# Experts in 64 full and 8 mixed slots, rows padded to 64, with each expert's weights as one long row per partition

## The reference

```python
cw = _combine_weights(xt, gate_w)           # [T, 16], 4 entries of a row are not zero
out = jnp.zeros_like(xt)
for e in range(16):
    a = _swiglu(xt @ expert_up_w[e].T)      # 512 -> 2 * 352 -> 352
    out = out + cw[:, e:e + 1] * (a @ expert_down_w[e].T)   # 352 -> 512
out = out + _swiglu(xt @ shared_up_w.T) @ shared_down_w.T
```

## Time and profile before

| | us |
|---|---|
| median of 3 runs (lowest, highest) | 1310.31 (1309.14, 1313.19) |
| span of the profiled execution | 1306.4 |
| PE busy | 1264.5 (97%) |
| DVE busy | 872.4 (67%) |
| ACT busy | 375.1 (29%) |
| POOL busy | 340.0 (26%) |
| TensorE clock over the span, of full speed | 0.989 |

### The profile page before, as it was taken

The page is one execution under the profiler, slowest core; times in us unless marked ns, Lnnn a source line. Parts: engine busy times, 40 slices in busy tenths (PEclk is TensorE's granted clock), DMA queues, the critical chain, the costliest instruction groups (busy, mean ns, idle before and its releaser), DMA issues.

```text
span 1306.4 us, 27873 instructions
## 1 busy us (share of the span) xinstructions
PE 1264.5 (97%) x8725; PEld 787.1 (60%) x8726; DVE 872.4 (67%) x2430; ACT 375.1 (29%) x822; POOL 340.0 (26%) x398
## 2 busy tenths in 40 slices
PE   8969999999999999999999999999999999999997
PEld 7857778777775555444444555555555555555553
DVE  4897688768768465262111777777777777777774
ACT  4745655645553333210000111111111111111111
POOL 1301234313242231225651112121212122121212
PEclk9989999999997999999999999999999999999999
DMA  5524944743643694585467456666665656564420
GB/s 163 95 47 99 157 94 101 166 105 85 138 109 114 169 199 116 124 274 199 182 211 246 85 130 138 134 137 137 137 139 133 135 132 136 127 139 72 75 49 9
DMA packets 208516, 171.09 MB, mean 131 GB/s; under 512 B 71472, under 2 KB 160560, under 8 KB 208432
## 3 DMA queue, kind: packets, MB, share of 16 engines
q1 hardware_dynamic: 135056, 114.16, 33.9%
q0 software_dynamic: 16496, 34.23, 13.4%
q10 hardware_dynamic: 56880, 21.54, 7.9%
HBM read 91.06 MB, written 82.73 MB: 133 GB/s over the span
## 4 chain that ended last, share of the span: by engine, by line
PE 55%; DVE 2%; issue 0%; DMA 0%; POOL 0%; ACT 0%; DVEq 0%; POOLq 0%
PE pD L2314 15%; PE pG L2289 14%; PE pU L2298 14%; PE pG L2246 3%; PE pU L2246 3%; PE pD L2265 3%; PE pU L2240 1%; PE pD L2260 0%; DVE ups L2187 0%; DMA out<-y,ix 0%; DVE w L1887 0%; DVE w L1888 0%; DVE route_keep L1886 0%; POOL out L2079 0%; DVE qf L1899 0%
## 5 line engine op out<-in xcount | busy, mean ns | idle before, releaser
L2187 DVE STREAM_TRANSPOSE ups<-a 32x96 f32<-32x96 f32 (+1 forms) x1248 | 326.1, 261 | 42.5
L2079 POOL DMA_INDIRECT out<-y,ix x79 | 123.0, 1557 | 479.1 <-ACT y L2140 319.4
L2314 PE MATMUL pD<-w,ups 128*128 (+1 forms) x474 | 216.6, 592 | 0.7 <-DVE ups L2187 0.7
L2289 PE MATMUL pG<-w,xsT 128*128 x632 | 199.9, 458 | 0.0
L2298 PE MATMUL pU<-w,xsT 128*128 x632 | 199.9, 459 | 0.0
L2289 PEld LDWEIGHTS pG<-w,xsT 128*128 128x128 f32 x632 | 119.5, 189 | 88.4 <-issue 37.4
L2298 PEld LDWEIGHTS pU<-w,xsT 128*128 128x128 f32 x632 | 120.1, 190 | 66.9
L976 PE MATMUL pProj<-front_region 128*128 128x256 f32 x624 | 154.8, 391 | 2.2 <-ACT front_region L711 1.6
L2314 PEld LDWEIGHTS pD<-w,ups 128*128 128x128 f32 (+1 forms) x474 | 90.0, 190 | 93.2 <-issue 76.8
L976 PEld LDWEIGHTS pProj<-front_region 128*128 128x128 f32 x624 | 113.3, 191 | 20.1 <-ACT front_region L711 2.1
L2140 ACT ACTIVATE y<-pD,wq 128x512 f32<-128x512 f32 x79 | 54.3, 687 | 247.0 <-PE pD L2314 234.1
(11 more groups left out here) (258 smaller groups left out, 1661.8 us busy)
## 6 DMA issues: line engine op xcount, KB each, us to landing
w<-in_up_T SPq DMA_DIRECT2D x16, 1408.0 KB
slot_rows<-zeros SPq DMA_DIRECT2D x79, 266.0 KB
xs<-slot_rows ACTq DMA_DIRECT2D x316, 64.0 KB
w<-in_down_T SPq DMA_DIRECT2D x16, 512.0 KB
front_region<-in_L_attn_hidden_states SPq DMA_DIRECT2D x16, 256.0 KB, 3.6
x2r<-in_L_attn_hidden_states SPq DMA_DIRECT2D x16, 256.0 KB, 4.5
partial_sums<-x2r SPq DMA_DIRECT2D x16, 256.0 KB, 2.9
x_normed<-x2n SPq DMA_DIRECT2D x16, 256.0 KB, 2.0
```

The costliest lines, as they stand in the source:

```text
L2079: pool.indirect_dma_start(out=flat, out_offset=bass.IndirectOffsetOnAxis(ap=ix[1 - par][:, 0:1], axis=0), in_=y[1 - par][:, :], in_offset= ...
L2187: dve.transpose(aT[par][B * to:B * to + B, 0:n, rows], a[rows, 0:len(IC) * P].rearrange("p (c n) -> p c n", c=len(IC))[:, 0:n, B * to:B * ...
L2289: mm = pe.matmul(pG[0][:, 0:I], xsT[par][:, k, :], w[:, bass.ds(slot, 1), 2 * I * k:2 * I * k + I], start=(k == 0), stop=(k == DC - 1))
L2314: mm = pe.matmul((pYlast if end(q) else pYq)[:, :], aT[1 - par][0:m, c, :], down[0:m, :, UPW + D * c:UPW + D * (c + 1)], start=(c == 0), s ...
```

## The change

**64 full and 8 mixed slots.** Each expert's count is rounded up to halves of 64 rows. Two halves of one expert make a full slot. Where an expert has an odd half, that half goes to a mixed slot, which holds two halves of two experts. There are always 64 full slots (NF) and 8 mixed ones (NM), NQ = 72. Slot q is mixed where q % 9 = 7. The list of slots is rebuilt: `lists` holds for the full slots the expert, its load and its buffer, for the loads which expert comes and until when its buffer is taken, and for the halves of the mixed slots the expert.

**Mixed slots.** PE multiplies each half with its own weights: `project` and `bring_down` issue two matmuls, with 64 stationary columns and 64 result partitions each, where a full slot has one. The weights of both halves come from `wm`, a view of `front_region` (free by then). ACT issues their loads, `load_mixed(m)`, at the end of its body of slot 9m, for the mixed slot 9m + 7. POOL adds a mixed slot's rows in two DMAs, one for each half, the second behind the first.

**Weights.** `in_expert_T` holds an expert as [128, 4352]: per partition one row. `load_expert` takes 128 rows of 15360 bytes, and 96 of 2048: 1920 KB and 192 KB.

**The rest.** The slots are written out without a loop. DVE makes the lists in five steps (`list_dve`) between the gated products of the shared expert's third group. Positions need 15 small operations in place of 6, and 6 more over [128, 256].

```diff
+def load_expert(eng, buf, rows, loaded):
+    eng.dma_start(buf[:, 0:UPW + 2 * D], rows[:, 0:UPW + 2 * D]).then_inc(loaded, 16)
+    eng.dma_start(buf[0:IC[2], UPW + 2 * D:UPW + DNW], rows[0:IC[2], UPW + 2 * D:UPW + DNW]).then_inc(loaded, 16)
...
-NQ = K * T // P + E - 1
+HR = P // 2
+NF = K * T // P
+NM = E // 2
+NQ = NF + NM
+STEP = NQ // NM
+MIXED = STEP - 2
...
+    wm = region[:, 0:2 * (UPW + DNW)].rearrange("p (h n) -> p h n", h=2)
...
                 if gr == 2:
-                    for s in range(3):
+                    sp.wait_ge(s_routed, 1)
+                    for s in range(NS):
                         sp.wait_ge(s_scat[1], 16 * (24, 28, 32)[s])
...
+                for h in range(2 if is_mixed(q - 1) else 1):
+                    to = ixm[h] if is_mixed(q - 1) else ix[1 - par]
+                    least(pool, s_add, 16 * (adds_before(q - 1) + h))
+                    pool.indirect_dma_start(out=flat, out_offset=bass.IndirectOffsetOnAxis(ap=to[:, 0:1], axis=0),
+                                            in_=y[1 - par][:, :], in_offset=None, bounds_check=T - 1, oob_is_err=False,
+                                            compute_op=ALU.add).then_inc(s_add, 16)
...
+            def load_mixed(m):
+                for h in range(2):
+                    load_expert(act, wm[:, h], weights_from(act, "mixed", 2 * m + h), s_wm)
...
+                if q % STEP == 0 and q < NQ:
+                    if first(q):
+                        act.wait_ge(s_routed, 1)
+                    load_mixed(q // STEP)
...
+                if gr == 2 and c < 5:
+                    list_dve(dve, c)
...
+            def project(out, rows, q, weights, at):
+                if is_mixed(q):
+                    for k in range(DC):
+                        for h in range(2):
+                            half = slice(HR * h, HR * h + HR)
+                            mm = pe.matmul(out[half, 0:I], rows[:, k, half], wm[:, h, 2 * I * k + at:2 * I * k + at + I],
+                                           start=(k == 0), stop=(k == DC - 1))
+                    return mm
```

More of the change, by code:

```diff
@@ L1781, with is_mixed, before_mixed, adds_before @@
 NE = E + 2
-NQ = K * T // P + E - 1
-assert NQ % 2 == 1
-NS = 3
-def routing(nc, es, counts, scratch, lg, xall, pos, qslot, qexp, tiles_to, s_pos, s_read, s_routed, route, s_xall):
+HR = P // 2
[4 more added lines that the diff above has]
+MIXED = STEP - 2
+NS = 3
+def is_mixed(q):
+    return q % STEP == MIXED
+def before_mixed(q):
+    return max(0, (q + STEP - 1 - MIXED) // STEP)
+def adds_before(q):
+    return q + before_mixed(q)
+def block_of(q):
+    return NF + q // STEP if is_mixed(q) else q - before_mixed(q)
+assert sorted(block_of(q) for q in range(NQ)) == list(range(NQ))
+assert all(q == i + (i + 1) // 8 for q in range(NQ) if not is_mixed(q) for i in [block_of(q)])
+def routing(nc, es, counts, scratch, lg, xall, pos, lists, s_pos, s_read, s_routed, route, s_xall):
     def sb(name, shape, dt=F32):
@@ L1871, in route_dve @@
                                     cnt[:, :, :].rearrange("p e t -> p (e t)"), 0.0, ALU.mult, ALU.add))
[L1872 to L1877, removed]
@@ L1914, in experts @@
+    return route_act, route_pool, route_pe, route_dve, list_dve
+def experts(nc, es, wex_d, xs_d, acc_d, x2n_d, xT_d, lg, pos, lists, region, wsh, route, sh, out):
     N = GN
@@ L1936, in experts @@
     wq, ix = [sb(f"wq{i}", [P, 1]) for i in range(2)], [sb(f"ix{i}", [P, 1], I32) for i in range(2)]
+    ixm = [sb(f"ix_mixed{i}", [P, 1], I32) for i in range(2)]
     def bank(n):
@@ L2121, in body @@
                     load_rows(1, 1)
-                if not (isinstance(q, int) and q >= NQ - 2):
+                if q < NQ - 2:
                     load_rows(q + 2, par)
@@ L2180, in turn_gated @@
                 dve.wait_ge(s_a, q + 1)
-                if not (isinstance(q, int) and q < 2):
-                    dve.wait_ge(s_yp, q - 1)
+                least(dve, s_yp, q - 1)
                 for to in range(BLOCKS):
@@ L2334, in program @@
         pos = es.enter_context(nc.sbuf_tensor("pos", [P, NT, K], I32))
-        qslot = es.enter_context(nc.sbuf_tensor("qslot", [1, NQ], I32))
-        qexp = es.enter_context(nc.sbuf_tensor("qexp", [1, NQ], I32))
-        tiles_to = es.enter_context(nc.sbuf_tensor("tiles_to", [1, E], I32))
+        lists = {name: es.enter_context(nc.sbuf_tensor(f"list_{name}", [1, n], I32)) for name, n in (
+            ("slot", NF), ("load", NF), ("expert", NF), ("source", E), ("until", E), ("mixed", E))}
         xs_d = nc.dram_tensor("slot_rows", (NQ * P, RW), F32, kind="Internal").ap()
```

294 lines of the change are left out of this document (184 added, 110 removed).

## The result

The changed kernel takes **1357.88 us** (median; 1353.59 to 1360.23) where the kernel before, on the same chip, takes 1310.66 (1309.14 to 1313.19): a ratio of 1.036 with a 95% interval of 1.034 to 1.038, slower. The prediction of 1298.8 us, on the faster side, was wrong, and the time lies above its range of 1262 to 1342.

What follows compares the result with a forecast made beforehand. PE was taken to bound the slots, 7.32 us each. -51.2 + 5.1 + 31 + 3.6 = -11.5 made a span of 1294.9 and a time of 1298.8 us, -0.9%; range 1262 to 1342.

Steps and rivals of the forecast that it cites:

- Seven slots fewer, -51.2: On PE's path in the slots: 79 slots become 72, each 7.32 us of PE, so -51.2 us.
- Mixed slots on PE, +5.1: Half-width pairs run side by side at the price of one; four width changes of 0.16 us in eight slots: +5.1 us.
- The rival of halves in series: In mixed slots the halves run one after the other on PE, 58.6 us more, 1357.4 us in all; chance 0.06.
- The rows behind the mixed weights, +31: On ACT's queue rows land after 4.33 MB of mixed weights and come late: 7 x 4.4 us = +31.
- The rows' own end: After the mixed weights, one add's bytes take 1.3 us and the rows, 256 KB in runs of 512 bytes, 1.2.
- 2.6 + 0.4: Behind each mixed load: rows turned 2.6 us after PE wants them, plus 0.4 for DVE's turns and gated product.
- SP's load beside it: An SP load falls into the mixed load's stretch with chance 0.45 and takes about 3 us: 1.4 a load.
- the bound of 77 us: Upper bound for late rows behind seven mixed loads: 11 us each, with 3 us for SP's load in every one.
- Adds: POOL's second add in each mixed slot: 0 in the steady part, +3.6 us at the end.
- As a rival the adds: Long weight runs hold up POOL's adds, deciding from about 10 us an add: 1339.8 us; chance 0.26.
- The tail, +3.6: At the end, the last slot but one is mixed; its second add stands ahead of the last one: +3.6 us.
- Ahead of the slots, 0: More position operations before the scatter, 4.8 us, hidden by 6.5 us of cover before PE's first gate product: 0.

Runs made afterwards that it cites:

- nomix: Changed kernel with mixed weights loaded only for the first mixed slot; the seven later ones multiply with those: 1268.61 us, ratio 0.968.
- after_few: Changed kernel with adds of only 16 of a slot's 128 rows from the tenth slot on, all waits kept: 1349.65 us, ratio 1.029.
- swap: Changed kernel with the mixed load issued right behind the next body's row and number loads, from the second pair on: 1323.11 us, ratio 1.009.
- nosp: Changed kernel with SP's expert loads cut to two transfers of 32 bytes a partition from the fourth expert on: 1325.38 us, ratio 1.011.
- early: Changed kernel with mixed weights in six pieces of 0.66 MB, at the ends of bodies -1 to 4 of each nine: 1310.20 us, ratio 0.999.
- b_long: Kernel before with only the weights' layout changed: one long row per partition, two transfers, 79 slots, no mixed slot: 1311.12 us, ratio 1.001.
- short: Changed kernel with every expert's weights back in two arrays and three transfers of shorter runs: 1360.41 us, ratio 1.040.
- half: Changed kernel with only the first half's weights, 2.16 MB of 4.33, loaded for the seven later mixed slots: 1300.77 us, ratio 0.992.
- four pieces: Changed kernel with mixed weights in four pieces of 1.08 MB at the ends of bodies 0, 2, 3 and 4 of each nine: 1285.88 us, ratio 0.980.

## Why the prediction was wrong

**Seven slots fewer, -51.2.** Right: gates of full slots are 7.31 us apart, and `nomix`, which keeps the 72 slots, is 42.2 us faster than the kernel before; -51.2 + 5.6 + 6.1 makes -39.5, and the spans differ by 39.0.

**Mixed slots on PE, +5.1.** Right: the halves run side by side. The chain of waits has 16 records of a mixed gate product in 2.52 us where 8 of a full one take 2.37, and each mixed slot costs 0.70 us more, 5.6 in all. The rival of halves in series falls; that its 1357.4 us is the time measured is chance.

**The rows behind the mixed weights, +31: the step that failed.** It cost 84.7, 12.1 a load in place of 4.4. Place and mechanism were right, as `nomix`, `after_few` and `swap` show, and the rate nearly so (385 GB/s on the mean while weights move, against 400 taken). What was wrong were the sizes of its parts, three of them by 2 to 3 us a load each:

- *The rows' own end.* 256 KB were taken at 1.2 us, 1.3 with an add's bytes apart. With two slots' rows in line and an add beside them the last stretch takes 4 to 5 us, at 86 to 209 GB/s. Without SP's loads PE stands still for 5.7 us a load (5.6 in the gap shown), where 2.6 + 0.4 was predicted.
- *The cold clock.* Not in the sum at all. Behind the waits the gate product ran at 1.2 GHz for most or all of its length, in the seventh gap, with 4.1 us of wait just before it, for 5.06 us in place of 2.37. That is 2.0 us a gap in the changed kernel, 13.9 in all, and 2.4 in `nosp`, 16.5 in all. A gap costs more than its idle time. From the chain of waits:

```profile
1286.74 5.06 PE pG L2406 x8
```
- *SP's load beside it.* The price was 3 us and the chance 0.45, 1.4 a load; measured 4.7 and six of seven, 4.0 a load. The chance was the worse of the two. SP's loads come when an expert's last product is done, which here is mostly in the slots 9m + 2 and 9m + 6, and the fixed place of `load_mixed` lies 7.4 us ahead of the first of these. Taking them as spread evenly over the slots was the error; the bound of 77 us, which has SP's load in every one, was nearer.

**Adds.** 0 in the steady part was nearly right for the changed kernel (`after_few` gains 8.2 us), because the rows mostly end later. Only in the fifth stretch does an add come first: PE waits 4.3 us for silu, and silu for a mixed slot's second add, issued at 1110.40, behind which DVE goes on at 1120.88. The wait of PE, from the same view as above:

```profile
PE pG L2406 <- ACT g L2235: 5.4, 3, 4.3
```

As a rival the adds had the right kind of delay: one of 12.1 us holds up `early`, while 9.56 holds up nothing in the kernel before, with the prediction's point of 10 us between. The reason was wrong: `b_long` and `short` show that the length of the runs does not matter. The Trainium skill (DMA: Bandwidth & Descriptors, Queues, rings and completion order) says that a DMA engine changes rings only at the end of a packet. The profile of the changed kernel counts 189,344 of its 193,565 packets under 8 KB. The other 4,221 fit the 4,096 long runs, each a packet of its own; the profile of the kernel before has 84 such packets. What I worked out from the rule, 4.9 us more for an add beside them, the trace does not bear out: 8.76 against 9.56. Where an add took 12 us (`early`), 0.66 MB on a second ring stood beside SP's 2.16.

The Trainium skill (DMA: Bandwidth & Descriptors, Where 436 GB/s comes from) gives about 358 GB/s a core, half of what a stack of HBM gives two cores, as HBM's limit. The mean of seven windows from 876 to 890 us is 385, so the trace differs here too. The slower rate would not have explained the loss either: by the prediction's estimate it makes 9 of the missing 54 us.

**The tail, +3.6.** 6.1. The mixed slot's second add is as predicted, 3.46 us. The last add also ends later: 8.5 us from its issue to the end of the span, against 6.2:

```profile
1336.35 1.56 POOL L2182 DMA_INDIRECT out<-y,ix_mixed  x1 [6.55 <-ACT y L2245]
1339.81 1.55 POOL L2182 DMA_INDIRECT out<-y,ix_mixed  x1 [1.91 <-DMA out<-y,ix_mixed]
1343.40 1.56 POOL L2182 DMA_INDIRECT out<-y,ix  x1 [2.03 <-DMA out<-y,ix_mixed]
```

It does so in `nomix` too (8.5 us from 1258.85), so the mixed loads are not the reason; which it is was not tried.

**Ahead of the slots, 0.** Right: the first gate product starts at 718.66 us, 718.44 before.

Together -51.2 + 5.6 + 84.7 + 0.5 (the first load's stretch) + 6.1 = +45.7, and the spans differ by 45.5.

**What stays open.** How the 8.0 us of a load without SP's share out between place in line and full engines (`swap` takes 34.8 us, but moves the next rows too, and what is left there is in part for adds). What tells the long gaps of `half` from its short ones. And why, with four pieces, the same meeting costs 13.5 us in one nine and nothing in another.

## What to carry to other kernels

A transfer of several MB is not hidden by a mean share of 64% on the DMA engines: what counts is what has to come through behind it on the same queue within one slot's slack, and what else starts in the same stretch. Where two waits run side by side, here rows and adds, the one that ends first comes to light when the other is gone. Look up when the other queue's loads start, stage by stage, before taking a chance for the meeting; then cut the transfer into pieces, put them into the bodies that hold no other load, and give the adds one buffer more (here 1357.9 to 1275.5 us with the same bytes). And price a gap on PE with the slow clock behind it.

## What the runs showed of the hardware

- Four row loads of 64 KB, whose issues take 2.0 us on ACT's queue elsewhere, take 6.9 behind 4.33 MB of outstanding weights on the same queue, and the longest single issue took 10.3. Without the mixed loads (`nomix`) the longest is 1.3, without SP's (`nosp`) 5.8. Silu and the scaling stand behind them on ACT. The view of that line (issues, ns least/median/most, first and last start in us):

```profile
L2208 ACTq DMA_DIRECT2D xs<-slot_rows x288: 309/453/10251, 705.2 to 1313.1; - x144
```

- DMA engines that are full by share (1.07 to 1.21) moved 180 to 209 GB/s with rows in runs of 512 bytes and adds; at shares of 0.98 to 1.06 they moved 336 to 415 with weights among them.
- PE, still from 886.7 on, had a granted clock of 0.93 in the window from 888 and 0.50 from 890; at work again from 896.32, it had 1.00 in the window from 900.
- A transfer in runs of 15,360 bytes and one in runs of 2,048 and 2,816 bytes cost the same in both kernels: 1311.1 against 1309.1 us, 1357.9 against 1360.4.
